# Packing adjacency words from the int32 buffer: TensorE reads it as float16, ScalarE copies the packed words, VectorE reads them from SBUF

## What is computed

```
h  = relu(layernorm(x))
Wh = (h @ W) in 4 heads of 32
e[i,j,head] = leaky_relu(s_src[i] + s_dst[j], 0.2) where adj[i,j] > 0, else -9e15
x  = x + elu(softmax_j(e) @ Wh)
h  = relu(layernorm(x))
x  = x + (max over the neighbours j of row i of h[j], 0 where there is none)
```

## Time and profile before

| what | value |
|---|---|
| median of 3 runs | 566.72 us (566.58 to 567.52) |
| span of the profiled execution | 568.4 us |
| VectorE busy | 414.2 us (73%), 1683 instructions |
| GpSimd busy | 364.5 us (64%), 390 |
| TensorE busy | 366.3 us (64%), 2583 |
| ScalarE busy | 302.0 us (53%), 747 |
| conversion (L682) | 64 x 1902 ns |
| second block begins | about 361 us |

### The profile page before, as it was taken

One profiled execution on the slowest core, in us unless ns is written; L12 is line 12 of the kernel. 1 busy time (PEld: TensorE's weight loads), 2 busy tenths in 40 slices (PEclk: granted clock), 3 DMA queues, 4 the chain that ended last, 5 costly groups with the idle time before them and its releaser, 6 DMA issues. The chain is left out here.

```text
span 568.4 us, 9640 instructions
## 1 busy us (share of the span) xinstructions
PE 366.3 (64%) x2583; PEld 272.3 (48%) x2598; DVE 414.2 (73%) x1683; ACT 302.0 (53%) x747; POOL 364.5 (64%) x390
## 2 busy tenths in 40 slices
PE   1955367696768784984927373387766676667763
PEld 1723234363536463642917372155544565545553
DVE  7998896989968998798686768365656565565562
ACT  1988356465666766762020223465656565565661
POOL 5944377175777575676768521577777777777771
PEclk9979587797968797887665776567788778787687
DMA  8999868977989899761222100112222222332321
GB/s 265 390 282 425 349 229 296 329 277 258 369 316 342 338 342 359 288 225 40 52 52 39 44 28 28 46 53 56 57 62 58 64 62 67 69 66 68 72 69 38
DMA packets 36776, 97.59 MB, mean 172 GB/s; under 512 B 6896, under 2 KB 23536, under 8 KB 28528
## 3 DMA queue, kind: packets, MB, share of 16 engines
q1 hardware_dynamic: 18272, 71.51, 32.7%
q0 software_dynamic: 9984, 21.11, 15.8%
q10 hardware_dynamic: 8464, 4.33, 2.8%
HBM read 90.49 MB, written 6.42 MB: 171 GB/s over the span
## 5 line engine op out<-in xcount | busy, mean ns | idle before, releaser
L662 POOL DMA_INDIRECT G<-wh_table,idx x156 | 160.3, 1028 | 83.7 <-issue 45.0
L1284 POOL DMA_INDIRECT G<-h_table,idx x156 | 148.0, 949 | 52.4 <-issue 40.3
L682 ACT ACTIVATE adjb<-adjf 128x2048 bf16<-128x2048 int32 x64 | 121.7, 1902 | 48.2 <-PE psf L783 36.6
L1366 DVE TENSOR_TENSOR_SCAN S<-Fl,S,psf 128x128 f32<-128x128 f32 x117 | 56.1, 480 | 72.5 <-PE psf L1329 64.5
L1329 PE MATMUL psf<-identf,G 128*128 128x128 f32 x156 | 59.4, 380 | 61.8 <-DMA G<-h_table,idx 61.0
L1308 ACT COPY Sb<-psf 128x128 f32<-128x128 f32 x156 | 41.6, 267 | 81.3 <-PE psf L1335 80.3
L1344 PE MATMUL psf<-Sb,OL 128*128 128x128 f32 x312 | 79.8, 347 | 0.0
L782 PE MATMUL psf<-adjb,packw 128*128 128x512 bf16 x241 | 73.3, 457 | 9.1 <-ACT adjb L682 5.8
L1329 PEld LDWEIGHTS psf<-identf,G 128*128 128x128 f32 x156 | 26.2, 168 | 91.5 <-DMA G<-h_table,idx 89.2
L884 PE MATMUL psf<-E,OQ 128*128 128x64 f32 (+2 forms) x312 | 47.9, 326 | 26.6 <-DVE E L1124 26.6
L1294 ACT ACTIVATE dg<-identb,keep 128x128 bf16<-128x128 bf16 x156 | 63.0, 404 | 2.8 <-PEq L446 2.8
(11 more groups left out here) (142 smaller groups left out, 649.6 us busy)
## 6 DMA issues: line engine op xcount, KB each, us to landing
adjf<-in_adj_dram SPq DMA_DIRECT2D x64, 1024.0 KB, 9.2
G<-wh_table,idx POOLq DMA_INDIRECT x156
G<-h_table,idx POOLq DMA_INDIRECT x156, 2.5
wh_table<-OQ ACTq DMA_DIRECT2D x8, 272.0 KB, 4.8
xsf<-in_x_dram SPq DMA_DIRECT2D x4, 512.0 KB, 7.2
out_dram<-rows_out SPq DMA_DIRECT2D x32, 64.0 KB
h_table<-h1b ACTq DMA_DIRECT2D x2, 384.0 KB, 3.2
h_table<-h1b ACTq DMA_DIRECT2D x2, 256.0 KB, 2.3
```

The source lines that it names most:

```text
L662: pool.indirect_dma_start(G[:, plan.at[k] + b, :], None, wh_table, bass.IndirectOffsetOnAxis(ap=idx[:, n:n + 1], axis=0)).then_inc(gathere ...
L682: nc.scalar.activation(adjb[:, t % 2, c:c + N // 2], adjt[:, m % NA, :], ACT.Copy, accum_out=rc[:, t, m % 2:m % 2 + 1]).then_inc(adj_bf, 1)
L1284: pool.indirect_dma_start(G1[:, n % NG, :], None, h1_table, bass.IndirectOffsetOnAxis(ap=idx[:, n:n + 1], axis=0)).then_inc(found[n % NG], 16)
L1366: V.tensor_tensor_scan(S[:, n % 5, :], Fl[:, n % 3, :], ps[:, 1 + n % 2, 0:P], start, ALU.mult, ALU.max).then_inc(scan_done, 1)
```

## The change

TensorE's pack reads the int32 buffer itself: the low half of each int32, seen as float16 with a stride of two, is zero or the smallest float16 number, 2^-24. The diagonals become 2^(8+k) in float16, and the column number c is scaled by 2^-25, so that every word is 2^-25 times what it was. A buffer of `adj` is free when the tile before last in it is packed. The conversion, `adjb` and `rc` are gone. ScalarE copies each packed tile from PSUM to one of four SBUF buffers `words`, with its row sums in `sums`; VectorE takes the words from there. TensorE packs, and ScalarE copies, two tiles further than TensorE packed before. "This row has no edge" is read from the aggregate's first softmax sum, and the test for edges that did not fit compares sums of bits.

```
         adjt = sbl("adjf", [P, NA, N // 2], I32)
-        adjb = sbl("adjb", [P, 2, N], BF16)
...
                 if m >= NA:
-                    sp.wait_ge(adj_bf, m - NA + 1)
+                    sp.wait_ge(packed, (m - NA) // 2 + 1)
...
-            nc.gpsimd.iota(cnum[:, :], ...).then_inc(consts, 1)
-            nc.gpsimd.memset(ones_b[:, :], 1.0).then_inc(consts, 1)
+            ch.step(nc.gpsimd.iota(cnum[:, :], ...))
+            nc.gpsimd.tensor_scalar(cnum[:, :], cnum[:, :], 2.0 ** -12, None, ALU.mult).then_inc(consts, 1)
+            nc.gpsimd.memset(ones_b[:, :], 2.0 ** -13).then_inc(consts, 1)
...
-            def convert(t):
-                for m in (2 * t, 2 * t + 1):
-                    act.wait_ge(adj_in[m % NA], 16 * (m // NA + 1))
-                    if m % 2 == 0 and t >= 2:
-                        act.wait_ge(packed, t - 1)
-                    c = (m % 2) * (N // 2)
-                    nc.scalar.activation(adjb[:, t % 2, c:c + N // 2], adjt[:, m % NA, :], ACT.Copy,
-                                         accum_out=rc[:, t, m % 2:m % 2 + 1]).then_inc(adj_bf, 1)
+            def copy_words(t):
+                act.wait_ge(packed, t + 1)
+                if t >= NW:
+                    act.wait_ge(words_used, plan.last[t - NW] + 1)
+                nc.scalar.activation(words[:, t % NW, :], ps[:, t % 2, :], ACT.Copy, accum_out=sums[:, t:t + 1]).then_inc(words_copied, 1)
...
-                if g == 1:
-                    convert(0)
...
-            convert_to(words_free(-1, POINTS - 1) + 2)
+            copy_words_to(2)
             for k in range(NBT + 4):
-                convert_to(words_free(k, 0) + 2)
+                copy_words_to(words_free(k, 0) + 2)
...
             def pack(t):
-                pe.wait_ge(adj_bf, 2 * t + 2)
                 if t >= 2:
-                    pe.wait_ge(words_used, plan.last[t - 2] + 1)
+                    pe.wait_ge(words_copied, t - 1)
                 o = ps[:, t % 2, :]
                 for k in range(BITS):
-                    nc.tensor.matmul(o, packw[:, k, :], adjb[:, t % 2, k * C:(k + 1) * C], start=(k == 0), stop=False)
+                    m = 2 * t + k // 4
+                    if k % 4 == 0:
+                        pe.wait_ge(adj_in[m % NA], 16 * (m // NA + 1))
+                    bits = adjt[:, m % NA, (k % 4) * C:(k % 4 + 1) * C].bitcast(F16).rearrange("p (c h) -> p c h", h=2)[:, :, 0]
+                    nc.tensor.matmul(o, packw[:, k, :], bits, start=(k == 0), stop=False)
...
+            pack_to(2)
             for k in range(NBT + 2):
...
-                pack_to(words_free(k, 0))
+                pack_to(words_free(k, 0) + 2)
...
-                    dve.wait_ge(packed, t + 1)
-                    words = ps[:, t % 2, :].rearrange("p (m g f) -> p f g m", g=GR, f=F)
+                    dve.wait_ge(words_copied, t + 1)
+                    words_t = words[:, t % NW, :].rearrange("p (m g f) -> p f g m", g=GR, f=F)
...
-                yield from apart(V.tensor_copy(wi[:, 0:nu * K].rearrange("p (u k) -> p u k", u=nu), src))
+                yield from apart(V.tensor_scalar(wi[:, 0:nu * K].rearrange("p (u k) -> p u k", u=nu), src, 1.0 / WORD, None, ALU.mult))
...
+                mark(V.tensor_scalar(high[:, bl].bitcast(I32), jq[:, 0, 0:S].bitcast(I32), 255 << 23, None, ALU.bitwise_and))
...
-                yield from apart(V.tensor_reduce(none[:, g], rc[:, g, :], AX, ALU.add))
-                yield from apart(V.tensor_scalar(none[:, g], none[:, g], 0.0, None, ALU.is_equal))
                 dve.wait_ge(ag_ready, tl[-1] + 1)
+                mark(V.tensor_scalar(none[:, g], ag[:, 0:nt, D], 0.0, None, ALU.is_equal))
```

More of the change, by code:

```diff
@@ L355 @@
 BIG = 1e30
+WORD = 2.0 ** -25
 class Plan:
@@ L500, in edge_attention @@
         m3 = sbl("m3", [P, 2, U, 3, H], BF16)
-        rc = sbl("rc", [P, T, 2])
+        sums = sbl("sums", [P, T])
+        words = sbl("words", [P, NW, C])
+        high = sbl("high", [P, NB])
+        totals = sbl("totals", [P, 4])
         none = sbl("none", [P, T])
@@ L713, in _, with copy_words_to @@
             nc.scalar.copy(s_all[:, :, :], whx[:, :, D + H:D + 2 * H]).then_inc(s_copied, 1)
[L714 to L720, removed]
-            convert_to(words_free(-1, POINTS - 1) + 2)
+            copied_to = -1
+            def copy_words_to(last):
+                nonlocal copied_to
+                while copied_to < min(last, T - 1):
+                    copied_to += 1
+                    copy_words(copied_to)
+            copy_words_to(2)
             for k in range(NBT + 4):
-                convert_to(words_free(k, 0) + 2)
+                copy_words_to(words_free(k, 0) + 2)
                 f = k - 4
@@ L824, in pack_to @@
                 nonlocal packs
-                while packs < last:
+                while packs < min(last, T - 1):
                     packs += 1
                     pack(packs)
+            pack_to(2)
             for k in range(NBT + 2):
@@ L1240, in _ @@
                 take_words(k, 3)
-            step(V.tensor_scalar(last_q[:, :], meta[:, :, 2], 0.0, None, ALU.is_gt))
-            step(V.tensor_reduce(missed[:, 0:1], last_q[:, :], AX, ALU.add))
-            step(V.tensor_reduce(missed[:, 1:2], rc[:, :, :].rearrange("p t c -> p (t c)"), AX, ALU.add))
-            step(V.tensor_tensor(missed[:, 2:3], missed[:, 1:2], missed[:, 0:1], ALU.subtract))
+            dve.wait_ge(words_copied, T)
+            n = mark(V.tensor_scalar(none[:, :], sums[:, :], 2.0 ** 24 * WORD, None, ALU.is_ge))
+            m = mark(V.tensor_scalar(sums[:, :], sums[:, :], 1.0 / (C * WORD), -(C - 1) / 2.0, ALU.mult, ALU.add))
+            mark(V.tensor_reduce(totals[:, 1:2], high[:, :], AX, ALU.add))
+            need(n)
+            mark(V.tensor_reduce(totals[:, 2:3], none[:, :], AX, ALU.add))
+            need(m)
+            n = mark(V.tensor_reduce(totals[:, 0:1], sums[:, :], AX, ALU.add))
+            need(n)
+            step(V.tensor_scalar(totals[:, 1:2], totals[:, 1:2], 1.0 / C, None, ALU.mult))
+            step(V.tensor_copy(missed[:, 0:3], totals[:, 0:3]))
             step(V.tensor_scalar(keep[:, :], kq[:, :], 0.0, None, ALU.is_gt))
@@ L1312, in _ @@
             pe.wait_ge(ones_ready, 2)
-            nc.tensor.matmul(ps[:, 6, 0:1], onesf[:, :], missed[:, 2:3], start=True, stop=True).then_inc(miss_done, 1)
+            nc.tensor.matmul(ps[:, 6, 0:3], onesf[:, :], missed[:, 0:3], start=True, stop=True).then_inc(miss_done, 1)
             for n in range(NB + 5):
@@ L1353, in _ @@
             dve.wait_ge(miss_done, 1)
-            ch.step(V.tensor_copy(missed[:, 3:4].bitcast(I32), ps[:, 6, 0:1]))
+            ch.step(V.tensor_copy(missed[:, 0:3], ps[:, 6, 0:3]))
+            ch.step(V.tensor_tensor(missed[:, 1:2], missed[:, 0:1], missed[:, 1:2], ALU.subtract))
+            ch.step(V.scalar_tensor_tensor(out=missed[:, 2:3], in0=missed[:, 0:1], scalar=2.0 ** 24, in1=missed[:, 2:3], op0=ALU.is_ge, op1=ALU.add))
+            ch.step(V.tensor_tensor(missed[:, 2:3], missed[:, 1:2], missed[:, 2:3], ALU.add))
+            ch.step(V.tensor_copy(missed[:, 3:4].bitcast(I32), missed[:, 2:3]))
             for n in range(NB + 7):
```

27 lines of the change are left out of this document (14 added, 13 removed).

## The result

The changed kernel is slower: 589.96 us median of 4 runs (583.81 to 596.18) against 567.12 for the kernel before beside it (566.58 to 569.14). The direction was forecast, the size was not: 573.7 us was said, with a range up to 581.

A forecast was written before the change was run, and what follows sets the result against it. VectorE sets the pace to about 162 us, from about 190 us the loop of GpSimd's gathers, bias, ScalarE's exp and weighting. 11.2 - 4.2 = +7.0 us on 568.4 gives 575.4, less 1.7 is 573.7 us; range 566.5 to 581.

The forecast's parts named there:

- The head of the program: +11.2 us: Start of the program: VectorE's first words wait for ScalarE's copy behind the projection, 32.8 in place of 21.60 us.
- about 11 us for the copy L684: Sign of a right forecast: VectorE's first MAX8 near 33 us, behind a wait of this length.
- Words from SBUF: 0: VectorE's MAX8 of 128 words: 280 ns from PSUM, 281 ns from SBUF (int32), so no change.
- Rival C: VectorE's strided SBUF reads of words cost 0.77 ns per element more, +6.7 us, later ones hide: 580; chance 0.10.
- Loads. ... I cost it at nothing: Adjacency buffers freed by a pack, not a conversion, equally far ahead of VectorE's use: 0 us.
- rival B: TensorE's packs stand still for loads, VectorE behind them: +2.8 to +5.7 us, about 578; chance 0.20.
- B's own second sign: Ahead of VectorE's selection: L1090 waits longer if TensorE stands still for loads; no size given.
- ScalarE's conversions gone: -4.2 us: GpSimd's waits for ScalarE's exp: 6.90 falls by 3.2, 4.89 by 1.0; bounds 2 and 6 for the two.
- its second step: Gain from ScalarE's removed conversions; wrong if the 11 us delay is still whole, or gone, at the first block's end.
- Packing from int32: TensorE's nine matmuls per tile reading every other half word: no change; bounds no change to twice 1.89 us of eight.
- Rivals A and D: A: gather and ScalarE waits shrink, 562, chance 0.11. D: no change, MAX8 cheaper or waits give 7.0 us, 566.7, chance 0.07.

The follow-up runs named there:

- e4: Kernel before with one added wait, holding VectorE's first words back until the projection is done: 705.45 us, ratio 1.0153 to the kernel before.
- e14: Kernel before with VectorE's first words held back until the projection is done, run again on another occasion: 696.12 us, ratio 1.0181.
- e12: Changed kernel with each group's words side by side in SBUF and a fifth load buffer, late first words left in: 693.1 us, ratio 1.0107.
- e5: Changed kernel with early copy of tile 0, words side by side and a fifth load buffer: 684.68 us, ratio 1.0002 to the kernel before.
- e6: Changed kernel plus MAX8 and COPY at several strides at the block's end: from SBUF, stride 4 words costs MAX8 0.7 ns more per element, from PSUM nothing.
- e13: Changed kernel with early copy of tile 0 and a fifth load buffer, strided words left in: 692.9 us, ratio 1.0133 to the kernel before.
- e8: Changed kernel with early copy of tile 0 and words side by side, four load buffers: 689.18 us, ratio 1.0079 to the kernel before.
- e9: Changed kernel with a fifth buffer for half tiles of adjacency and nothing else: 583.22 us, ratio 1.0277 to the kernel before.
- e11: Changed kernel with early copy, words side by side, fifth buffer, and packs and copies back two tiles later: 570.68 us, ratio 1.0016.
- e10: Changed kernel with early copy, words side by side and fifth buffer, again with more rounds on another chip: 572.48 us, ratio 1.0035.
- e7: Changed kernel unedited, run again on a chip where the kernel before takes 684.14 us: 702.72 us, ratio 1.0268.

## Why the prediction was right and wrong

**"The head of the program: +11.2 us": right.** 10.7 was measured (32.30 against 21.60), with the wait of "about 11 us for the copy L684" where it was said. It was also right that everything later hangs behind it: the first gather is 11.6 us late, and e4 and e14 show the price of such a wait alone, 1.5% and 1.8%. In the changed kernel it was less, 1.05% (e12 against e5), though the intervals touch.

**"Words from SBUF: 0": wrong.** This is the larger failed step. It took the 281 ns of an int32 MAX8 as the price of reading from SBUF; those elements lie side by side, the words 16 bytes apart. The term was put at nothing and measured 92 ns on each MAX8 of 128 words (372 against 280 before). The right row stood in the same group, L1137 against L1104, and gave 0.77 ns per element; e6 measured 0.7 for MAX8 itself. Rival C priced it at 380 ns and 6.7 us on the path; 372 ns was measured, 11.3 us over all 168. It was given 0.10 because "MAX8 from PSUM has the same stride and no surcharge". That is true, and e6 shows that it says nothing about SBUF. Whether the later ones hide, as C had it, is not settled: e13 loses 9 us with the stride alone, some 4 either way, and both 6.7 and 11.3 lie in that.

**"Loads. ... I cost it at nothing": wrong.** The same stalls that ScalarE had borne came to TensorE, which has others behind it: rival B, given 0.20 and 2.8 to 5.7 us. With the fifth buffer e8's loss went away in e5, 5.3 us. B's own second sign, a longer wait of VectorE for the selection, did not come (5.9 us for L860 in the changed kernel, 7.6 for L858 before); the waits stand elsewhere. One place where the loads do harm is seen on TensorE, VectorE and ScalarE in turn:

```profile
226.25 1.86 PE L783 MATMUL psf<-adjf,packw 128*128 128x512 f16 x4 [2.46 <-DMA adjf<-in_adj_dram]
230.68 1.89 PE L783 MATMUL psf<-adjf,packw 128*128 128x512 f16 x4 [2.56 <-DMA adjf<-in_adj_dram]
...
233.04 0.67 PE L847 MATMUL psf<-m,Rm 128*128 128x12 bf16 x19
```

```profile
233.75 0.40 DVE L1160 TENSOR_REDUCE dq<-psf 128x76 f32<-128x228 f32 x1 [2.62 <-PE psf L847]
235.35 0.22 DVE L1092 COPY meta<-psf 128x60 f32<-128x60 f32 x1 [1.21 <-PE psf L860]
```

```profile
233.73 0.86 ACT L732 ACTIVATE h1b<-xsf,bias,rstd 128x128 f32<-128x128 f32 x2
...
236.21 2.42 ACT L741 CAST OQ<-psf 128x1024 f32<-128x1024 bf16 x3 [1.62 <-PE psf L870]
```

Two packs wait 2.46 and 2.56 us for half tiles. VectorE stands 2.62 and 1.21 us for the matmuls behind them, and ScalarE's cast, which GpSimd's weighting waits for, 1.62 us. With the fifth buffer alone (e9) the same place has one wait of 1.82, VectorE's second wait is 0.40 and the cast's 0.95.

VectorE's longest wait for TensorE comes later, and it is not simply the loads:

```profile
242.96 1.07 PE L783 MATMUL psf<-adjf,packw 128*128 128x512 f16 x4 [1.73 <-DMA adjf<-in_adj_dram]
...
246.19 8.80 PE L886 MATMUL psf<-E,OQ 128*128 128x64 f32 x40 [1.85 <-DVE E L1127]
254.78 6.41 PE L898 MATMUL psf<-G,OQ 128*128 128x132 f32 x38
...
265.46 0.39 PE L838 MATMUL psf<-X,tri 128*128 128x6 f32 x2
```

```profile
265.88 0.17 DVE L1041 COPY X<-psf 128x6 f32<-128x6 f32 x1 [5.89 <-PE psf L838]
```

The kernel before, at the same work:

```profile
234.87 4.68 PE L884 MATMUL psf<-E,OQ 128*128 128x64 f32 x40
239.39 4.49 PE L896 MATMUL psf<-G,OQ 128*128 128x132 f32 x38
```

L886 starts behind a wait of 1.85 us for VectorE's own E, not behind a load. It and L898 then take 15.2 us for the same 78 matmuls that took 9.2, and these 6.0 us are the whole of VectorE's 5.89. The granted clock was 1.00 until 245 us and 0.50 from 245 to 258 (the lower of TensorE's two levels), where the kernel before had 1.00 from 233 to 248. It fell while TensorE stood still for E, some 2 us after it had stood 1.73 us for a half tile. Between the same two gathers of GpSimd (232.92 to 267.55 before, 242.25 to 280.29 now) 3.4 us are lost, 1.6 of them in the wait for ScalarE's exp (5.80 against 4.19), 0.9 in a longer wait for indices and the rest among the gathers.

The fifth buffer does not cure this stretch: e9 has the same 8.79 us for L886, the same wait of VectorE (5.94) and the same loss between those gathers (38.05 us, where the kernel before had 34.63). What goes with it is the place of the packs. These 40 matmuls took 8.56 to 8.80 us in every trace with the packs two tiles further on, and 4.68 in the four without (the kernel before, e4, e14, and e11, which has all else of the repaired kernel):

```profile
235.72 4.68 PE L889 MATMUL psf<-E,OQ 128*128 128x64 f32 x40 [0.32 <-DVE E L1130]
```

In e11 the stretch between those gathers takes 35.50 us. What that is worth at the end is not shown: e10 and e11 do not differ clear of the noise. Nor is it shown how much of the 5.3 us of the loads goes by the clock; the mean granted clock of the runs was 0.689 in e8, 0.698 in e5 and 0.707 in the kernel before on that chip.

**"ScalarE's conversions gone: -4.2 us": right where it was looked for, and nothing of it at the end.** The waits of GpSimd for ScalarE's exp fell from 4.89 to 3.59 and from 6.90 to 5.35, 1.3 and 1.6 where 1.0 and 3.2 were forecast, 2.9 in place of 4.2. The part of the 6.90 that a late conversion made was really there and did go:

```profile
225.66 0.86 ACT L734 ACTIVATE h1b<-xsf,bias,rstd 128x128 f32<-128x128 f32 x2
...
226.97 2.42 ACT L743 CAST OQ<-psf 128x1024 f32<-128x1024 bf16 x3 [0.45 <-ACT h1b L734]
```

L734 began 2.93 us after its bias (222.73), behind a conversion whose half tile was late; L732 now begins 0.20 after it (233.53 to 233.73). But the cast waits 1.62 in place of 0.45, for the transposes that the loads held back on TensorE. So late loads did have somebody behind them in the kernel before, by way of ScalarE. In e11 the two waits are 3.59 and 4.02, 4.2 less together, just as forecast. In the changed kernel the next wait, at 277.03, is 5.80 where 4.19 was, behind the slow stretch of TensorE, so some 1.2 us are left in all. By the prediction's own sign its second step failed (the delay at the end of the first block is 14.3 us, "still whole"), because the other losses came on top. With the three losses repaired no gain shows: 1.0002, 1.0035, 1.0016. Part of the reason is seen in e11 (on another chip of the faster kind), beside the kernel before: the first gather at 165.13 (161.92 before) is 3.2 us late, the one at 233.00 (232.92) is level, and the second block begins 1.6 late; ScalarE's freed time made up a delay and no more. Where those 3.2 us come from is open, but for 1.1 at the first words. ScalarE had been made 101 us less busy (302.0 to 200.8), off the path for the most part.

**"Packing from int32": right.** Eight matmuls take 1.96 us (1.89 in the earlier trace rows); reading every other half word costs nothing that shows.

**"Rivals A and D": neither.** The gather waits did fall, to 4.7 us in total, but VectorE then waited for TensorE instead; MAX8 did not get cheaper.

**The size.** 11.2 - 4.2 = 7.0 us was forecast. With terms as the traces and runs give them it would have been 10.7 for the head, 6.7 to 9 for the stride, 5.3 for the loads and -4.2 to -1.2 for ScalarE: 18.5 to 23.8, against 16.6 to 21.7 by the ratio's interval. The forecast took its rivals as alternatives, one of which might come true; B and C both did, on top of it, and the range held only one at a time. Two more things stay open: why the changed kernel's runs spread over 583.8 to 591 us when those of the kernel before spread over 2.6, and therefore where the 5 to 7 us lie by which its other runs exceed the profiled one, in which 13.9 us were found.

## What to carry to other kernels

Ask of work that is taken off an engine not how busy the engine was but who stood behind it: 101 us less on ScalarE bought nothing, and waits for loads, moved from it to TensorE, cost some 5 us until a fifth buffer took most of them away. When an operand moves between memories, find a row with the same memory and the same stride, not only the same instruction; and where a buffer's reader changes, look at the first use of all, where a copy queued behind a long start-up held the whole program back for 11 us. When an engine waits long for another, look at the granted clock over the work it waits for before blaming what stands ahead of it: VectorE's longest wait for TensorE here was 78 matmuls at the lower clock. All three losses could be removed (one copy earlier, the rearrangement put into the copy's own read, one buffer more), and what was left was the time of the kernel before, not a gain.

## What the runs showed of the hardware

- VectorE's reads of f32 from SBUF cost 0.7 ns more per element at strides of 16 bytes and more for MAX8 (384 against 295 ns for 128), and 45 ns more for a COPY of 128. The same reads from PSUM cost nothing more at any stride up to 32 bytes, nor do ScalarE's (597 ns for 128x512 either way), so the engine that reads PSUM is the one to do the rearranging.
- Matmuls on float16 halves of int32 words, at a stride of two, run like those on bf16 side by side (1.96 and 1.89 us for eight of 512 columns).
- The same program takes 567 to 569 us on some chips and 684 to 695 on others. On the slower ones the profile shows waits for which it names no releaser of the program (VectorE in e7: 54.2 us in 4 times), and the mean granted clock of the kernel before is lower, 0.69 to 0.71 against 0.78. The cause is open; the intervals of the ratios of the same edit overlap between the two kinds (1.0338 and 1.0268 for the change, 1.0035 and 1.0002 for all three edits).
- The same 40 matmuls of 64 float32 columns took 8.80 us at a granted clock of 0.50 and 4.68 at 1.00.
